# A spectral tower on one core: the x transform as one call per group, and a first layer on two row tiles

## The reference, cut to what matters

```
h = layer_norm(x @ fc0_w + fc0_b)
for i in range(4):
    x_ft = rfft2(h)                                   # 12 ky of either sign, 12 kx are kept
    out[:, :, :12, :12]  = einsum(x_ft[:, :, :12, :12], w1[i])
    out[:, :, -12:, :12] = einsum(x_ft[:, :, -12:, :12], w2[i])
    h = layer_norm(irfft2(out) + conv1x1(h))
    if i < 3: h = gelu(h)
h = mlp(h)
```

## Time and profile before

| what | value |
|---|---|
| three runs | 3276.86, 3277.98, 3285.92 us |
| median | 3277.98 us |
| span of the profiled execution | 3279.2 us |
| busy: PE, DVE, ACT | 2937.9, 2145.9, 1950.3 us |
| granted TensorE clock, mean | 0.966 |

### The profile page before, as it was taken

How to read it: one execution, slowest core, us unless ns; L and a number is a source line. 1 busy time by engine, 2 the same in 40 slices (tenths; PEclk the granted TensorE clock), 3 DMA queues, 4 the chain that set the end, 5 groups by cost and what they waited for, 6 DMA issues and landing times.

```text
span 3279.2 us, 82177 instructions
## 1 busy us (share of the span) xinstructions
PE 2937.9 (90%) x32240; PEld 1867.7 (57%) x32240; DVE 2145.9 (65%) x3954; ACT 1950.3 (59%) x2271; POOL 61.9 (2%) x81
## 2 busy tenths in 40 slices
PE   7888889999889999889999889999999987964994
PEld 3545466666666666666666544444444447952893
DVE  6888668888668888668888644454445434255457
ACT  6777656666556666556666457777777753422451
POOL 0000000000000000000000010000000001000000
PEclk9999999999999999999999999999999998986897
DMA  3422346544447544546544423111111000000000
GB/s 96 130 97 99 100 152 209 193 165 164 152 130 218 183 164 163 155 154 209 179 165 164 151 67 86 46 55 58 46 46 55 29 1 1 1 1 0 1 1 13
DMA packets 98093, 335.91 MB, mean 102 GB/s; under 512 B 29928, under 2 KB 61960, under 8 KB 62088
## 3 DMA queue, kind: packets, MB, share of 16 engines
q1 hardware_dynamic: 75400, 161.50, 16.4%
q10 hardware_dynamic: 18432, 134.23, 10.0%
q0 software_dynamic: 4096, 37.75, 5.3%
HBM read 179.29 MB, written 154.14 MB: 102 GB/s over the span
## 4 chain that ended last, share of the span: by engine, by line
PE 79%; DVE 11%; issue 5%; ACT 5%; DVEq 0%; SPq 0%; DMA 0%; ACTq 0%
PE pA L1291 15%; PE pA L1299 8%; PE pT L1385 8%; PE pT L1317 5%; PE pS L1328 5%; PE pD L1342 4%; PE pD L1374 4%; PE pD L1356 4%; PE pD L467 3%; PE pA L467 3%; PE pD L1263 3%; PE pA L1281 3%; PE pS L459 2%; PE pT L459 2%; DVE arena L1657 2%
## 5 line engine op out<-in xcount | busy, mean ns | idle before, releaser
L1624 DVE TENSOR_REDUCE small<-arena 128x32 f32<-128x1056 f32 x320 | 397.0, 1241 | 316.0 <-ACT arena L1461 311.3
L1291 PEld LDWEIGHTS pA<-conv_bd,h_in 128*128 128x128 f32 x4096 | 479.0, 192 | 109.4 <-issue 92.7
L1291 PE MATMUL pA<-conv_bd,h_in 128*128 128x128 f32 x4096 | 517.4, 280 | 8.6 <-DVE arena L1617 2.9
L1451 ACT COPY w_sb<-pA 128x1024 f32<-128x1024 f32 x256 | 259.8, 1015 | 393.0 <-PE pA L1299 343.3
L1638 DVE SCALAR_TENSOR_TENSOR w_sb<-w_sb,small 128x1024 f32<-128x1024 f32 x320 | 386.8, 1213 | 5.5
L1472 ACT ACTIVATE h_new<-pT,bet,gam 128x1024 f32<-128x1024 f32 x256 | 307.5, 1201 | 100.2 <-PE pT L1317 92.1
L1461 ACT ACTIVATE arena<-w_sb 128x1024 f32<-128x1024 f32 x320 | 339.3, 1060 | 13.4
L1317 PEld LDWEIGHTS pT<-cst,w_sb 128*128 128x128 f32 x2048 | 225.2, 143 | 144.5 <-issue 123.9
L1317 PE MATMUL pT<-cst,w_sb 128*128 128x128 f32 x2048 | 283.0, 282 | 23.2 <-DVE w_sb L1638 23.2
L1476 ACT COPY h_rows<-pS 128x1024 f32<-128x1024 f32 x256 | 257.1, 1004 | 64.9 <-PE pS L1328 64.6
L1328 PEld LDWEIGHTS pS<-cst,h_new 128*128 128x128 f32 x2048 | 228.5, 143 | 113.0 <-issue 71.6
(11 more groups left out here) (299 smaller groups left out, 3903.0 us busy)
## 6 DMA issues: line engine op xcount, KB each, us to landing
h_scratch<-h_new ACTq DMA_DIRECT2D x128, 1024.0 KB, 4.5
h_in<-h_scratch SPq DMA_DIRECT2D x128, 1024.0 KB, 5.1
y_scratch<-w_sb POOLq DMA_DIRECT2D x32, 576.0 KB, 8.4
y_in<-y_scratch SPq DMA_DIRECT2D x512, 36.0 KB
w_sb<-in_L_tok_w1r_dram POOLq DMA_DIRECT2D x8, 576.0 KB, 7.0
w_sb<-in_L_tok_w1i_dram POOLq DMA_DIRECT2D x8, 576.0 KB, 6.7
w_sb<-in_L_tok_w2r_dram POOLq DMA_DIRECT2D x8, 576.0 KB, 8.3
w_sb<-in_L_tok_w2i_dram POOLq DMA_DIRECT2D x8, 576.0 KB, 7.7
```

The source lines that it names most:

```text
L1291: pe.matmul(pA[:, c:c + 128], h_in[:, 1024 * n + c:1024 * n + c + 128], conv_bd[:], start=(j == 0), stop=False, skip_group_check=True)
L1624: dve.reduce_sum(var[n], sq[n % 2], axis=AX).then_inc(s["summed"], 1)
```

## The change

- **x transform.** One call `f2.0` does both images b. The output rows are b and real or imaginary part; both ky signs share 24 of 32 columns of one weight (12 kx for either sign). A call has 16 matmuls, of 13 and of 12 ky's width (416 and 384 columns), where two calls had 32 of 384 or 352. DVE turns 832 columns in one instruction. ACT packs in four instructions of 64 partitions, one for each sign and image; a pack takes its rows from either half of XF.
- **First layer.** `x_in` holds, for each of two images-pairs t, 48 columns and a one and zeros up to 64; four full transposes take the place of eight of 48 rows, and ACT copies 512 columns. fc0 and its bias stand twice, on rows 0 to 63 and 64 to 127, and `acc` multiplies 64 rows at t's row tile. The input of a group comes in two transfers of four pieces of 192 B per row. fc0 takes 34 transfers.
- **Orders.** The strings of "first" and "mid" are new for all three engines; in `into_last`, `f2.1-` and `pack.1-` go.

```diff
 ORDER = { "first": {
-        "PE": ("xt.0 turn.2- back.1- acc.0 back.2- turn.3- acc.1 back.3- acc.2 f1.0- turn.0 f1.1- acc.3 f2.0- back.0 "
-               "turn.1 f2.1-"),
-        "ACT": ("xt.0 gelu.2- back.1- acc.0 back.2- sq.0 gelu.3- acc.1 sq.1 back.3- acc.2 sq.2 gelu.0 acc.3 sq.3 "
-                "back.0 gelu.1 pack.0- pack.1-"),
-        "DVE": ("red.3- rs.3- scale.3- cen.0 cen.1 cen.2 red.0 rs.0 scale.0 red.1 f1.0- rs.1 f1.1- red.2 scale.1 "
-                "f2.0- rs.2 f2.1- scale.2"),
+        "PE": ("xt.0 turn.2- acc.0 back.1- acc.1 back.2- turn.3- acc.2 back.3- acc.3 f1.0- turn.0 f1.1- turn.1 f2.0- "
+               "back.0"),
+        "ACT": ("xt.0 gelu.2- acc.0 back.1- sq.0 acc.1 sq.1 back.2- gelu.3- acc.2 back.3- sq.2 acc.3 sq.3 gelu.0 "
+                "gelu.1 back.0 pack.0-"),
+        "DVE": ("red.3- cen.0 rs.3- cen.1 cen.2 scale.3- red.0 red.1 rs.0 rs.1 scale.0 f1.0- scale.1 f1.1- red.2 rs.2 "
+                "f2.0- scale.2"),
     "mid": {
-        "PE": ("i1.0 turn.2- back.1- acc.0 i1.1 turn.3- back.2- acc.1 back.3- acc.2 f1.1- turn.0 f1.0- acc.3 f2.0- "
-               "turn.1 f2.1- back.0"),
-        "ACT": ("gelu.2- back.1- acc.0 sq.0 gelu.3- back.2- acc.1 sq.1 back.3- acc.2 sq.2 gelu.0 acc.3 sq.3 pack.0- "
-                "gelu.1 back.0 pack.1-"),
-        "DVE": ("red.3- i1.0 rs.3- scale.3- cen.0 cen.1 i1.1 red.0 rs.0 scale.0 red.1 rs.1 f1.1- scale.1 red.2 f1.0- "
-                "rs.2 f2.0- cen.2 scale.2 f2.1-"),
+        "PE": ("turn.2- i1.0 acc.0 i1.1 back.1- acc.1 back.2- turn.3- acc.2 back.3- turn.0 f1.1- acc.3 f1.0- back.0 "
+               "turn.1 f2.0-"),
+        "ACT": ("gelu.2- acc.0 sq.0 back.1- acc.1 sq.1 gelu.3- back.2- acc.2 back.3- sq.2 gelu.0 acc.3 gelu.1 sq.3 "
+                "pack.0- back.0"),
+        "DVE": ("red.3- i1.0 rs.3- cen.0 scale.3- red.0 i1.1 rs.0 red.1 scale.0 rs.1 cen.1 scale.1 red.2 f1.1- rs.2 "
+                "f1.0- scale.2 cen.2 f2.0-"),
...
             def load_x(g):
-                sp.dma_start(x_in, src[g]).then_inc(s["x_loaded"], 16)
+                for t in range(2):
+                    sp.dma_start(x_in[:, :, t, 0:48], src[g, t]).then_inc(s["x_loaded"], 16)
...
                 def xt(n, g):
-                    for t in range(2):
-                        for xb in range(4):
-                            mm = pe.transpose(bank[0:48, 512 * t + 128 * xb:512 * t + 128 * xb + 128],
-                                              x_in[:, t, 48 * xb:48 * xb + 48], ident)
+                    for xb in range(4):
+                        mm = pe.transpose(bank[:, 128 * xb:128 * xb + 128], x_in[:, xb].rearrange("p t n -> p (t n)"), ident)
...
                         for t in range(2):
-                            mm = pe.matmul(pA[:, 512 * t:512 * t + 512], xT[:, t, 128 * n:128 * n + 128],
-                                           fc0.rearrange("p x o -> p (x o)"), start=True, stop=True)
+                            q = slice(64 * t, 64 * t + 64)
+                            mm = pe.matmul(pA[:, 512 * t:512 * t + 512], xT[q, 128 * n:128 * n + 128],
+                                           fc0[q].rearrange("p x o -> p (x o)"), start=True, stop=True)
...
-                def f2(b, g):
+                def f2(n, g):
                     for part in range(2):
-                        for j in range(4):
-                            for t in range(2):
-                                rows, first = slice(64 * t, 64 * t + 64), part if j < 2 else 0
-                                slot = (M1 + 1 if part else 0) + (1 - part if j >= 2 else 0)
-                                out = bank[32 * j:32 * j + 32, 512 * t + 32 * first:512 * t + 384]
+                        for b in range(2):
+                            for ri in range(2):
+                                for t in range(2):
+                                    rows, m = slice(64 * t, 64 * t + 64), 64 * b + 32 * ri
+                                    slot = (M1 + 1) * part
+                                    out = bank[m:m + 32, 512 * t + 32 * part:512 * t + 32 * (M1 + 1)]
...
-                def pack(b, g):
-                    act.copy(spec_g[:, bass.ds(g, 1), b].rearrange("p g t (q k) -> p (g t) q k", k=KX),
-                             XF[b].rearrange("p (t q k) -> p t q k", t=2, k=NQ)[:, :, :, 0:KX]).then_inc(s["packed"], 1)
+                def pack(n, g):
+                    for w in range(2):
+                        for b in range(2):
+                            half = XF[64 * b:64 * b + 64].rearrange("p t (q k) -> p t q k", k=NQ)
+                            ins_ = act.copy(spec_g[64 * w:64 * w + 64, bass.ds(g, 1), b].rearrange("p g t (q k) -> p (g t) q k", k=KX),
+                                            half[:, :, w:w + M1, KX * w:KX * w + KX])
+                    ins_.then_inc(s["packed"], 1)
...
-                def f2(b, g):
-                    dve.wait_ge(s["packed"], at("packed", ph, L, g, b + 1))
-                    dve.transpose(XF[b].rearrange("p (t n) -> p t n", t=2),
-                                  bank.rearrange("p (t n) -> p t n", t=2)[:, :, 0:384]).then_inc(s["d_free"], 1)
+                def f2(n, g):
+                    dve.wait_ge(s["packed"], at("packed", ph, L, g, 0) + 1)
+                    dve.transpose(XF, bank.rearrange("p (t n) -> p t n", t=2)[:, :, 0:NQ * (M1 + 1)]).then_inc(s["d_free"], 1)
```

More of the change, by code:

```diff
@@ L79, in constants @@
         for w, sign in enumerate((1, -1)):
-            f2[:, :, 0, w, 0, k], f2[:, :, 0, w, 1, k] = c, -t
-            f2[:, :, 1, w, 0, k], f2[:, :, 1, w, 1, k] = -sign * t, -sign * c
-    put("dft_x", f2.reshape(P, 8 * NQ))
+            f2[:, :, 0, 0, KX * w + k], f2[:, :, 0, 1, KX * w + k] = c, -t
+            f2[:, :, 1, 0, KX * w + k], f2[:, :, 1, 1, KX * w + k] = -sign * t, -sign * c
+    put("dft_x", f2.reshape(P, 4 * NQ))
     ix = np.zeros((2, 2, KX // 2, 2, 2, S))
@@ L130 @@
     "h_new":         (4, 0, 4, 4),
-    "x_in":          (16, 0, 0, 0),
+    "x_in":          (32, 0, 0, 0),
     "y_in":          (0, 0, 128, 128),
@@ L134 @@
     "stored":        (16, 0, 16, 0),
-    "packed":        (2, 0, 2, 0),
+    "packed":        (1, 0, 1, 0),
 }
@@ L157 @@
     },
     "into_last": {
[L159 to L164, removed]
+        "PE": ("i1.1 turn.2- back.1- i1.0 acc.0 turn.3- back.2- acc.1 back.3- acc.2 f1.1- f1.0- acc.3 f2.0- mix.0 "
+               "turn.0 fc1.0 turn.1"),
@@ L165 @@
+        "ACT": ("gelu.2- back.1- acc.0 sq.0 gelu.3- back.2- acc.1 sq.1 back.3- acc.2 sq.2 acc.3 sq.3 pack.0- mix.0 "
+                "fc1.0 fc1.1"),
+        "DVE": ("red.3- i1.1 rs.3- scale.3- i1.0 red.0 rs.0 scale.0 red.1 rs.1 f1.1- scale.1 red.2 f1.0- f2.0- mix.0 "
+                "turn.0"),
     },
@@ L269, in build @@
         TA = V.rearrange("p (h b c q) -> p b h c q", h=2, b=2, q=NQ)
-        XF = [arena[:, 5152 + 768 * t:5920 + 768 * t] for t in range(2)]
+        XF = arena[:, 5152:5152 + 2 * NQ * (M1 + 1)].rearrange("p (t n) -> p t n", t=2)
         conv_all = arena[:, 7744:8256]
@@ L971, in load_x @@
             def load_x(g):
-                src = ins["x"].rearrange("(g t b) y x c -> g (b y) t (x c)", t=2, b=2)
-                sp.dma_start(x_in, src[g]).then_inc(s["x_loaded"], 16)
+                src = ins["x"].rearrange("(g t b) y (x z) c -> g t (b y) x (z c)", t=2, b=2, x=4)
+                for t in range(2):
+                    sp.dma_start(x_in[:, :, t, 0:48], src[g, t]).then_inc(s["x_loaded"], 16)
             sp.dma_start(cst[:], ins["consts"][:, 0:NC_EARLY]).then_inc(s["cst_loaded"], 16)
             load_x(0)
[L977 to L980, removed]
+            sp.wait_ge(s["fc0_clear"], 1)
+            for t in range(2):
+                for x in range(16):
+                    q = 64 * t + 3 * x
+                    sp.dma_start(fc0[q:q + 3, x, :], ins["L0_tok_fc0_w"]).then_inc(s["fc0_loaded"], 16)
+                q = 64 * t + 48
+                sp.dma_start(fc0[q:q + 1], ins["L0_tok_fc0_b"].rearrange("(p x o) -> p x o", p=1, x=1).broadcast_to([1, 16, C])).then_inc(s["fc0_loaded"], 16)
             for j in range(4):
@@ L1191, in mix @@
                 alone(pe)
-                pe.wait_ge(s["packed"], (at("packed", p.ph, p.L, 0, 0) if half else at("packed", p.ph, p.L, NG // 2, 0)) + 2)
+                pe.wait_ge(s["packed"], (at("packed", p.ph, p.L, 0, 0) if half else at("packed", p.ph, p.L, NG // 2, 0)) + 1)
                 alone(pe)
@@ L1344, in f1 @@
                     send(mm, "f1", ch, g)
-                def f2(b, g):
-                    bank = bank_of("f2", b, g)
+                def f2(n, g):
+                    bank = bank_of("f2", n, g)
                     alone(pe)
                     for part in range(2):
-                        for j in range(4):
-                            for t in range(2):
-                                rows, first = slice(64 * t, 64 * t + 64), part if j < 2 else 0
-                                slot = (M1 + 1 if part else 0) + (1 - part if j >= 2 else 0)
```

(16 more changed lines are left out.)

33 lines of the change are left out of this document (16 added, 17 removed).

## The result

The changed kernel takes 3177.58 us (median of 4 runs, 3173.61 to 3180.27) where the kernel before takes 3277.55 beside it: a ratio of 0.968 with a 95% interval of 0.967 to 0.970. The forecast was 3154 with a range of 3120 to 3205, so the sign and the range held and the time was 24 us longer than forecast.

What follows compares the result with a forecast made beforehand. PE bounds the middle body nearly alone; in the first layer DVE and PE wait on each other. Middle 100, first layer 27, into_last 1.5, start -4: 124 us off 3279, 1 less against the median, gives 3154, range 3120 to 3205.

Steps and rivals of the forecast that it cites:

- f2 as one call: PE, each of 63 bodies: one merged call takes 1.61 us by columns for two of 1.55 and 1.54, saving 1.5.
- the rival of 3.1: f2 on PE: the merged call takes as long as two, 3.1 us; total 3243; chance 0.06.
- the two new stalls of the middle body: PE: i1.0 waits 0.3 us for DVE's f2 transpose, f1.1 some 0.5 for ACT's copy of back.3.
- the mix wait: Before six mixes: ACT packs first, so PE waits about 4.0 us behind f2, losing about 2.6 at each.
- the start: Kernel start: SP issues 17 more transfers at 0.31 us; 5.3 lost at most, 0 at least, 4 taken.
- The rival that the middle order stalls PE: Middle bodies: the new order stalls PE as the old did, 26.1 us a body; total 3197; chance 0.15.
- that of a first layer at 24.0: First-layer bodies stay at 24.0 us, DVE's chain of reductions and roots refilled by other waits; total 3180; chance 0.12.
- The clock's rival: First-layer bodies: PE, less busy, runs at 1.2 GHz throughout, losing 135 us; total 3317; chance 0.04.
- The sign that the forecast named: Outside the mixes: a granted clock falling below 0.9 would show the forecast wrong.
- The part on mix, start and loads: Six mixes lose about 2.6 us each, the start 4; input and activations' loads have time to land, costing nothing.
- a saving of 2.4: Middle body: PE's new order takes 24.3 us plus 0.8 stalls and 0.1 restarts, 25.2 for 27.64.
- DVE hides it: First-layer body: DVE becomes the bound at 22.2 us, so acc's 2.7 saved on PE is worth nothing by itself.

## Why the prediction was right, and where it was wrong

**Right in mechanism, and in the size of most parts.** f2 as one call at 1.58 (1.61 by columns; the rival of 3.1 is out), DVE's transpose 1.05, the pack 1.75 hidden on ACT, acc at 218.37 - 217.31 = 1.06 as two rounds (1.05), the two new stalls of the middle body, the mix wait of 4.2 (a loss of 3.0 each, where 2.6 was taken), the start of 3.9. The bodies came out within 0.2 us. The rival that the middle order stalls PE is out by the rows of i1.0 and f1.1; that of a first layer at 24.0 is out by its packs, although the time it gave, 3180, is near the one measured: a total can agree with a case that didn't occur. The clock's rival didn't occur here either: 1.00 in the first-layer body. It did in part in the two runs with a short acc in the old orders, at 0.93 in some of these bodies. The sign that the forecast named, a clock below 0.9 outside the mixes, did show: it comes with the stall behind the store and adds some 1.7 us to it in two bodies.

**The step that failed: loads were weighed, stores not.** The part on mix, start and loads asks whether the new order leaves the activations' loads time to land and never asks it of h_new's stores, which gate gelu. In the new order gelu.0 is ready about 10 us behind back.1's store (517.98 to 528.3), where it came 14.7 behind it before, and the y burst falls just ahead of that store. The sum lacks a term for it of some 10 us; the run with later stores gives it back. That run moves the burst and leaves the slack of about 10 us, in which the store then lands (4.4 us), so the shorter slack alone is not enough for the wait. Whether the burst ahead of the store would have been enough with the old slack was not run; 15.5 us to land against 14.7 of slack would make it under 1 us a body, an estimate.

**A term mis-sized: the middle body.** 25.2 forecast, 25.38 measured, against a saving of 2.4 taken: 2.26 in place of 2.4 is some 6.6 us over 47 bodies. The start's 4 was right, but 14 first-layer bodies at 1.91 would have gained 26.7 and 20.9 were seen: the head lost 1.9 more, which bodies 0.1 shorter than forecast made good.

**A reason that held in one kernel and not in the other.** "That PE became cheaper by 2.7 in acc is then worth nothing by itself: DVE hides it." Alone on the kernel before it is worth next to nothing, as written (0.2 us a body, 0.3 at full clock). But the sum took from this that the merged call brings the first-layer body to 22.2 whatever acc costs, and that fails: with the old acc it is 23.95. DVE's queue was counted full; in the new order red.0 and red.1 stand earlier, and their squares come in time only from the short first steps. So 22.2 came out right with the help of a saving that the forecast had counted as worthless there: that much of it is luck.

**What stays open.** The mixes themselves became 7.7 us shorter, which nothing in the forecast foresaw; in the profiles of kernels with the new orders they add up to between 116.0 and 118.6, in those of the three with the old orders to between 121.0 and 123.7, with no edit in mix itself. So it goes with the orders, by a path that no run here shows. Some 4 us of the short stretches are placed only in part. And why the clock fell behind some stalls of 2.1 to 2.3 us and not behind others stays open.

## What to carry to other kernels

When an order is remade, walk every buffer that an engine overwrites back to the transfer that last read it: write down the slack of stores as well as of loads, and look for bursts on other queues beside them. An edit's worth depends on the order around it, so a step "hidden" by another engine must be recounted in the new order: here two parts worth 0.1 and 0.2 us a body alone gave 1.9 together. At a drain (here mix) look at what stands between the last result and the copy that the next stage waits for; swapping two words was worth 16 us.

## What the runs showed of the hardware

- A 1 MB store landed in 3.9 us when four stores of 576 KB from another queue were issued 3.0 us behind it, and in 15.5 us when they were issued 1.7 us ahead of it.
- A stall of two microseconds can cost more than itself, and doesn't always: behind PE's gap of 2.26 us in the body of 29.3, the granted clock of the next 7 us was 0.76, a mean between 2.4 and 1.2 GHz, with PE busy 6.11 of them, and the body grew by 3.9; behind a gap of 2.13 us it was 1.00 and the body grew by 2.2. Without the stall it was 1.00.
- Relieving PE cost clock in one order and not in the other: with the short acc in the old orders, first-layer bodies alternated between 0.93 (24.3 us) and 1.00 (23.4 us); in the new orders they stayed at 1.00. PE was busy 18.3 us of the first, 17.0 of the second and 17.3 of the 22.1 in the new orders.
- Two row tiles of 64 rows with 128 columns of weights and 512 streamed columns each ran side by side: 1.06 us for what took 1.72 on full rows.
